# Layer 0 of a two-layer kernel: ScalarE's two x_dbl copies move behind the conv products and the decays, and TensorE's fold and dt products move to earlier steps of in_proj

## What is computed

```python
x  = hs @ in_proj_w.T                              # 768 -> 1536 channels, "in_proj"
xs = silu(depthwise_conv3x3(x) + conv_b)           # u
x_dbl = xs_seq @ x_proj_w.T                        # 1536 -> 48 + 4 + 4
dt, Bs, Cs = split(x_dbl)
delta = softplus(dt @ dt_w.T + dt_b)               # 48 -> 1536
dA  = exp(delta * A);  dBu = (delta * u) * Bs      # 4 states
states = associative_scan(dA, dBu)                 # along the tokens
y   = sum_n states_n * Cs_n + D * u
out = layernorm(y) @ out_proj_w.T;  x = x + out
```

## Time and profile before

| | |
|---|---|
| median of 3 runs | 3685.06 us (3684.29 to 3686.72) |
| the profiled execution, its own time | 3683.9 us |
| its span | 3682.1 us |
| PE busy | 3382.5 us, 92% |
| DVE busy | 2868.8 us, 78% |
| ACT busy | 2345.9 us, 64% |
| POOL busy | 2346.0 us, 64% |
| steady layer 0, one chunk | 153.7 us, in which PE 148.1, DVE 147.0, POOL 139.9, ACT 123.8 us busy |

### The profile page before, as it was taken

How to read it: one execution, slowest core, us unless ns; L and a number is a source line. 1 busy time by engine, 2 the same in 40 slices (tenths; PEclk the granted TensorE clock), 3 DMA queues, 4 the chain that set the end, 5 groups by cost and what they waited for, 6 DMA issues and landing times. The chain is left out here.

```text
span 3682.1 us, 39373 instructions
## 1 busy us (share of the span) xinstructions
PE 3382.5 (92%) x10888; PEld 1745.1 (47%) x10888; DVE 2868.8 (78%) x4117; ACT 2345.9 (64%) x4095; POOL 2346.0 (64%) x1557
## 2 busy tenths in 40 slices
PE   5875799999999999999999999998798999999999
PEld 4432234333343344334333343343346877767787
DVE  4469999999999988999999999998754345565532
ACT  1357787887878867877788777887535555443211
POOL 0139898999989978898998989999830001112211
PEclk7897799999999999999999999999899999999999
DMA  7244355555556545555555555555533223356654
GB/s 288 81 144 118 92 137 150 153 148 147 139 149 159 145 130 131 149 142 146 158 144 150 134 147 160 136 160 146 139 87 114 66 83 107 117 191 210 209 199 153
DMA packets 217179, 529.93 MB, mean 144 GB/s; under 512 B 24744, under 2 KB 45928, under 8 KB 214016
## 3 DMA queue, kind: packets, MB, share of 16 engines
q1 hardware_dynamic: 173952, 376.39, 32.5%
q0 software_dynamic: 43008, 151.02, 18.5%
HBM read 346.17 MB, written 80.48 MB: 116 GB/s over the span
## 5 line engine op out<-in xcount | busy, mean ns | idle before, releaser
L575 PE MATMUL p_in<-xn,win_v 128*128 128x512 f32 (+1 forms) x2304 | 1064.3, 611 | 125.4 <-ACT halo L766 83.0
L591 PE MATMUL p_op<-uy,wout_ring 128*128 128x512 f32 x2160 | 987.5, 606 | 39.0 <-DVE x_res L970 38.9
L935 DVE TENSOR_TENSOR_SCAN p_da<-p_da,state,g_ring 128x512 f32<-128x512 f32 x672 | 827.3, 1277 | 107.9 <-ACT p_da L725 70.3
L907 POOL TENSOR_TENSOR g_ring<-du,B_bc 128x2048 f32<-128x2048 f32 x192 | 870.7, 4535 | 16.7 <-DMA B_bc<-bc_scratch 1.8
L956 DVE SCALAR_TENSOR_TENSOR p_cv<-win_v,conv_w,p_cv 128x512 f32<-128x512 f32 x960 | 722.8, 753 | 87.9 <-ACT p_cv L787 67.0
L575 PEld LDWEIGHTS p_in<-xn,win_v 128*128 128x128 f32 x2304 | 440.8, 197 | 705.8 <-issue 705.8
L591 PEld LDWEIGHTS p_op<-uy,wout_ring 128*128 128x128 f32 x2160 | 401.1, 192 | 614.2 <-issue 539.9
L725 ACT ACTIVATE p_da<-delta,A 128x512 f32<-128x512 f32 x768 | 499.4, 682 | 12.5 <-ACT state L730 0.2
L941 DVE TENSOR_TENSOR g_ring<-p_da,C_bc 128x512 f32<-128x512 f32 x768 | 486.9, 675 | 0.0
L1387 PE MATMUL banks<-x_split,w_split 128*128 128x512 f32 x1152 | 458.9, 398 | 11.0 <-DVE x_split L1590 5.5
L1389 PE MATMUL banks<-x_split,w_split 128*128 128x512 f32 x1152 | 450.4, 391 | 0.0
(11 more groups left out here) (220 smaller groups left out, 4070.3 us busy)
## 6 DMA issues: line engine op xcount, KB each, us to landing
g_ring<-g_ring POOLq DMA_DIRECT2D x192, 512.0 KB, 5.6
win_v<-in_win SPq DMA_DIRECT2D x192, 384.0 KB, 3.1
wout_ring<-wout_scratch SPq DMA_DIRECT2D x184, 384.0 KB, 3.8
x_ring<-x_scratch SPq DMA_DIRECT2D x192, 256.0 KB, 2.7
q_scratch<-q_ring POOLq DMA_DIRECT2D x96, 256.0 KB, 2.5
x_split<-q_scratch SPq DMA_DIRECT2D x96, 256.0 KB, 3.4
out<-x_ring POOLq DMA_DIRECT2D x96, 256.0 KB, 3.0
x_res<-in_x SPq DMA_DIRECT2D x90, 256.0 KB, 4.5
```

The costliest lines, as they stand in the source:

```text
L575: last = nc.tensor.matmul(p_in[:, 0:n], WR[:, i % NW, t, :], XN[:, t, off:off + n], start=(t == 0), stop=(t == XT - 1))
L591: last = nc.tensor.matmul(p_op[:], OR[:, e % NO, k - h * HALF, :], ucol(c * K + k), start=(k == 0), stop=(k == K - 1))
L907: nc.gpsimd.tensor_tensor(G[:, i % NG], DU[:].unsqueeze(1).broadcast_to([P, NS, N]), BB[:], ALU.mult).then_inc(s_dbu, 1)
L935: nc.vector.tensor_tensor_scan(bank, bank, G[:, i % NG, n, :], init, ALU.mult, ALU.add)\
```

## The change

Only the order inside the handover slots changes. On ACT, copy 1 is issued behind the second conv product instead of ahead of the first, and copy 2 behind the states and the two decays instead of ahead of them. On PE, the fold stands ahead of step 1 of the six steps 0 to 5 (so behind the first) instead of ahead of step 3, and the first dt pair ahead of step 3 (behind the third) instead of ahead of step 4. No instruction is added or taken away, and DVE, POOL and SP keep their order.

```diff
@@ in_proj (PE)
                     for t in range(XT):
-                        if t == 3 and fold_of is not None:
+                        if t == 1 and fold_of is not None:
                             fold_xproj(fold_of)
-                        if t == 4 and pair_of is not None:
+                        if t == 3 and pair_of is not None:
                             delta_pair(pair_of, S)
@@ ScalarE's loop
-                    c = chunk_at(S, S_XP[2] + 1)
-                    if c is not None:
-                        act.wait_ge(s_xp, 2 * (c + 1))
-                        wait(act, s_bw, 16 * c)
-                        nc.scalar.activation(XD[:], p_dt[:, 0, :], ACT.Copy).then_inc(s_xe, 1)
                     if b is not None:
                         product(b, 0)
...
                         product(b, 1)
                     c = chunk_at(S, S_XP[2] + 1)
                     if c is not None:
-                        act.wait_ge(s_xf, c + 1)
-                        nc.scalar.activation(XD[:], p_dt[:, 1, :], ACT.Copy).then_inc(s_xd, 1)
+                        act.wait_ge(s_xp, 2 * (c + 1))
+                        wait(act, s_bw, 16 * c)
+                        nc.scalar.activation(XD[:], p_dt[:, 0, :], ACT.Copy).then_inc(s_xe, 1)
                     if i is not None:
                         keep_state(i, 0)
                         act.wait_ge(s_scp, 2 * i + 1)
                         decay(i, 2)
                         decay(i, 3)
+                    c = chunk_at(S, S_XP[2] + 1)
+                    if c is not None:
+                        act.wait_ge(s_xf, c + 1)
+                        nc.scalar.activation(XD[:], p_dt[:, 1, :], ACT.Copy).then_inc(s_xd, 1)
```

## The result

The changed kernel takes 3695.4 us (median of 7 runs, 3693.4 to 3698.8) against 3685.6 for the kernel before beside it (median of 7). The ratio is 1.0029, with a 95% interval of 1.0019 to 1.0039: slower by 9.8 us, where no change was forecast. The profiled execution is the longest of the seven, 3698.76 us with a span of 3697.0 (before 3682.1), so its trace shows 14.9 us more and not 9.8.

A forecast was written before the change was run, and what follows sets the result against it. No engine has much idle time; a wait chain from copy 1 to PE's second dt pair bounds the handovers. 8.0 + 4.2 - 10.5 = +1.7 us on 3685.06 gives 3686.8; own range 3681.7 to 3690.2, full 3677.0 to 3697.5.

The forecast's parts named there:

- rival 1: Ten steady handovers win nothing, as PE, busy 96% of a chunk, waits later instead: 3697.3 us, slower; chance 0.10.
- the steady handovers: Handovers of chunks 2 to 5 and 8 to 13: second dt pair 1.05 us earlier each, 10.5 us in all.
- One sign of being wrong: Forecast wrong if the steady chunk is 153.7 or 151.6 us, or the edges cost under 5 or over 18 together.
- the order of the edges: Handovers of chunks 0, 1, 6, 7, 14, 15: later copy 1 or 2 makes PE wait, 8.0 us lost.
- the term for PE's clock: Lower granted clock behind lengthened PE waits: 2.8 us in chunk 7, 1.4 in chunk 1; +4.2, ends 0 and 6.6.
- the second change of shape: PE's switch from in_proj steps to the second dt pair in a steady handover: 0.09 us, bounds 0 to 0.09.
- rival 2: Ten handovers turn into chunk 6's picture, POOL's add late, fold late, 0.6 us each: 3703 us, slower; chance 0.07.
- rival 3: DVE keeps the whole 2.15 us won at its first scan in ten handovers: 3675.8 us, faster; chance 0.08.
- Rival 4: Chunks 0, 1, 15 swallow their losses as the pipeline fills or drains: 3677.6 us, faster; chance 0.07.
- The failing step: PE's gaps of 1.4 to 2.0 us in chunks 0, 6 and 14: no clock loss behind them, 0 us.
- the rule on long gaps: Gaps where PE waits throttle its clock, so work behind starts cold; speaks against the change in chunks 1 and 7.

The follow-up runs named there:

- the filled run: Both halves in chunk 7's handover alone, plus four overwritten PE products ahead of the fold there, against the kernel before: 3685.3 us against 3684.8, ratio 1.0002.
- the filled changed kernel: Changed kernel plus overwritten PE products in waits: four in chunk 7's handover, two in each of four waits behind chunks 6 and 14; 3693.9 us, ratio 1.002.
- the earlier second pair: Kernel before with PE's new order everywhere, ACT's in the steady ten, second dt pair ahead of in_proj's last step, four softplus in a row: 3671.4 us, ratio 0.9959.

## Where the prediction held and where it failed

The measured 3695.4 us lies inside the full range, 3677.0 to 3697.5, and outside the forecast's own, 3681.7 to 3690.2. That the full range holds it is luck: it reaches so far up only for rival 1, in which the steady handovers win nothing, and they did win. The loss came from elsewhere and happened to be nearly as large. One sign of being wrong that was named beforehand came: the edges cost more than 18 us together, 22.6 in the trace and 9.8 + 9.2 = 19.0 by the median. Of the 8.1 us between the forecast's +1.7 and the measured +9.8, 1.3 stand at the steady handovers, 0.5 at the order of the edges and 6.3 at the term for PE's clock.

**The steady handovers: right, 0.13 us too large each.** The chain ran as told: copy 1 into the gap, fold without a wait, second pair by PE's own work, the rest 1:1 behind it. 0.92 was measured for 1.05, so 9.2 for 10.5. The mis-sized part, 0.10 of the 0.13, is the second change of shape: three steps between the pairs take 719.68 - 716.91 = 2.77 us, and 2.58 + 0.09 was put down, with 0 to 0.09 as its bounds. In the kernel before, the same extra was hidden behind the 0.88 us for which the pair waited; with ACT's half alone PE has its old order without that wait, and its second pair is at 7.46 too. The forecast gave DVE 3.1 us at the second scan; it is 3.33. Rivals 1, 2 and 3 fell by this: the chunk is 152.78 long, chunk 6's picture shows up nowhere in the ten (the fold stands right behind the first step), and DVE gave back what it had won. The Trainium skill ("Perfetto Trace Analysis", section Identifying the Most-Contended Engine) says which engine to work on first, the one with the highest occupancy; it doesn't say that a new order without less work wins nothing, as the prediction read it for rival 1. PE, the busiest here, kept its work (148.01 us for 148.08) and lost idle time (4.77 us for 5.62).

**The order's cost at the edges: right.** 8.0 was predicted; the traces give 8.5:

- Chunk 0: the second pair is 256.09 - 247.18 = 8.91 us behind in_proj's start, before 253.12 - 245.69 = 7.43, so +1.5 (predicted 1.3).
- Chunk 1: everything ahead of it is 2.23 late, the fold starts at 405.37 - 2.23 = 403.1, as predicted. With the 6.50 us from fold to second pair that a steady handover takes, that is +1.6 (1.5).
- Chunks 6 and 14: +0.84 each (0.6); for chunk 14 this is without the 1.69 of clock below.
- Chunk 7: +1.83 (1.8).
- Chunk 15: the first pair starts at 2580.96, 11.61 late by what is ahead, so 2569.35 against 2567.41: +1.9 (2.2).

Rival 4, that chunks 0, 1 and 15 would swallow their part, fell too.

**PE's clock: here the prediction failed.** It put +4.2, with 6.6 as the upper end. In the profiled execution it is what is left of the six chunks' loss, 22.6 - 8.5 = 14.1 us in layer 0, of which about 0.7 (chunk 0's +2.23 less its 1.5) is start-up that differs between executions. Two of its terms hold: behind chunk 7's wait 3.0 us were lost where 2.8 was predicted (1340.21 - 1338.34 = 1.87 from the fold to in_proj against 0.97 in the filled run, and 1347.52 - 1340.21 = 7.31 from there to the pair against 5.24; but only 1.7 behind the same 4.01 us with chunk 7 alone). Chunk 1 lost 413.67 - 405.37 = 8.30, less 6.50, so 1.8 where it was 1.4:

```profile
405.37 1.80 PE L581 MATMUL p_dt<-x_dbl,fold 128*128 128x512 f32 x2 [2.69 <-ACT x_dbl L807]
...
406.96 2.95 PE L575 MATMUL p_in<-xn,win_v 128*128 128x512 f32 x4
```

The failing step is "Chunks 0, 6 and 14 get gaps of 1.4 to 2.0, next to the row without a loss: 0". It looked only at the work directly behind the lengthened waits. Lost were 2.06 us in chunk 6 behind the handover, 1.69 in chunk 14's handover and 2.06 behind it, and 1.69 each ahead of and behind chunk 7's, 9.2 us in all. Most of these are stretches with the same waits as before, and a single trace in which they all run at full speed gives no upper bound. Chunk 14's handover, whose gap of 1.80 us was taken as harmless because of the 1.80 in the earlier trace rows, is the plainest. Chunk 6's stands ahead of it, behind the same wait:

```profile
1170.95 1.12 PE L581 MATMUL p_dt<-x_dbl,fold 128*128 128x512 f32 x2 [1.80 <-ACT x_dbl L807]
1171.92 1.67 PE L575 MATMUL p_in<-xn,win_v 128*128 128x448 f32 x4
...
2425.71 1.45 PE L581 MATMUL p_dt<-x_dbl,fold 128*128 128x512 f32 x2 [1.80 <-ACT x_dbl L807]
...
2426.95 3.08 PE L575 MATMUL p_in<-xn,win_v 128*128 128x448 f32 x4
```

The same two products (four records) took 1.67 us in the one and 3.08 in the other. So the length of the wait ahead doesn't decide by itself. The Trainium skill ("TensorE: Matmul & The Clock Gate", section A second HAM failure mode: psum-queue depth-cycling) states for a bf16 kernel that short, frequent idle times between groups of products can make the clock oscillate as well. The 7.08 us behind 0.49 agree in that a short wait is enough; that it is the same mechanism, no run shows. The prediction used only the rule on long gaps.

**Does the median hold it too?** Every execution's mean granted clock is on record. The seven of the changed kernel lie between 0.962 and 0.964, the 71 of the kernel before beside the experiments (without the one left out) between 0.964 and 0.970, on average 0.967 to 0.968. So the changed kernel gets less of the clock in every execution, not only in the profiled one. Among those 71, the eight at 0.966 have a median of 3688.7 us and the fourteen at 0.969 one of 3682.8, some 2 us for each 0.001. For the 0.004 between the two kernels that makes 8 to 9 us, an estimate from executions of the kernel before alone. It isn't a proof: the filled changed kernel rose to 0.966 and won 1.5 us, not 4 or 5.

**The sum.** With 9.2, 8.5 and the clock of the profiled execution the trace adds up: -9.2 + 8.5 + 14.1 + 1.5 = 14.9. The 14.1 is a difference; the slow stretches listed above make 3.0 + 1.8 + 9.2 = 14.0 of it, and chunk 0's 0.7 stands against 0.6 won back in small steps in chunks 1, 7 and 15. The median's 9.8 leaves 9.8 + 9.2 - 8.5 = 10.5 for the clock and what lies behind layer 0, against a forecast of 4.2.

**What stays open.** Why identical waits of 2.1 to 2.3 us are followed by the full clock in the kernel before and by the lower one in the changed kernel. Of the four in_proj runs behind the handovers of chunks 6 and 14 none was slow in the traces of the kernel before and of chunk 7 alone; one was with the steady handovers alone, two with the earlier second pair, three with ACT's half, and four with PE's half, with the edges alone and with the whole change. So nearly all slow ones stand behind a handover in a new order, but one does not, and behind such handovers ACT's half has one at full speed and the earlier second pair two. These are single traces, and no mechanism is shown.

## What to carry to other kernels

An idle engine ahead of an instruction costs only if the chain behind it is the one that ends last. Here PE's second dt pair was, and either half of the change brought it to the same place, so try the halves apart and keep the one that harms least elsewhere (3678.8 against 3695.4). A rule that suits ten of sixteen places should be made conditional on the place. And when a change lengthens PE's waits, take the clock's cost from more than the work directly behind them: in the trace it was the larger half of the loss (14.1 of 22.6 us), and about half of it stood in stretches that nobody had touched.

## What the runs showed of the hardware

- The same six products (twelve records) of 448 columns, behind waits equal to 0.03 us, took 4.75 or 6.44 us; the granted clock was 1.00 in the one window and 0.79 in the other. Six of 512 columns took 5.39 or 7.08 behind a wait of 0.49, and also behind one of 2.0.
- Products into a bank that is overwritten later, put into such waits, cost nothing (ratio 0.9999 in the kernel before) and kept the work behind them at full speed in each of the traces with them. They didn't lower the median beyond its interval.
- At the changes between in_proj's steps and the dt pairs PE lost 0.09 us ahead of the first pair and about 0.2 between the two (three steps in 2.77 for 2.58), which counts once PE is the chain. Whether the shape costs this or something else at these places, no run separates.
- The mean granted clock of executions of one kernel differed by 0.004 (0.965 and 0.969), and their times by 14.5 us (3677.0 and 3662.4). In 71 executions of the kernel before, 0.966 went with a median of 3688.7 us and 0.969 with 3682.8.
